# Perceiver megakernel, expert stage: two conditional parts on VectorE joined, and the third transposed group of the first token block issued half a weight group later

## The reference, cut to what matters

```python
scores = softmax(x2d @ gate_w.T)                  # [512, 8]
top_scores, sel = top_k(scores, 2)                # two experts for each of 512 tokens
routed_in = x2d[token_idx] * top_scores           # 1024 rows, sorted by expert
for e in range(8):
    xe = where(eid == e, routed_in, 0)
    h = silu(xe @ w1[e]) * (xe @ w3[e])           # 512 -> 1408
    out += h @ w2[e]                              # 1408 -> 512
x = x + scatter_add(out, token_idx)
```

## Time and profile before

| | |
|---|---|
| time, three runs | median 1844.7 us (1841.14 to 1847.6) |
| profiled execution | 1843.16 us, its span 1841.6 us |
| TensorE busy (matmul) | 1740.0 us, 94% of the span |
| VectorE busy | 1172.4 us, 64% |
| ScalarE busy | 982.1 us, 53% |
| GpSimd busy | 235.9 us, 13% |
| mean granted TensorE clock | 0.977 of full speed |
| expert stage | about 1499.7 to 1825.2 us of the span |

### The profile page before, as it was taken

How to read it: one execution, slowest core, us unless ns; L and a number is a source line. 1 busy time by engine, 2 the same in 40 slices (tenths; PEclk the granted TensorE clock), 3 DMA queues, 4 the chain that set the end, 5 groups by cost and what they waited for, 6 DMA issues and landing times. The chain is left out here.

```text
span 1841.6 us, 25720 instructions
## 1 busy us (share of the span) xinstructions
PE 1740.0 (94%) x9446; PEld 1428.0 (78%) x9446; DVE 1172.4 (64%) x2453; ACT 982.1 (53%) x2033; POOL 235.9 (13%) x138
## 2 busy tenths in 40 slices
PE   7999999999898989999999999999899879999996
PEld 5778888877787779999899989887455557778785
DVE  5777777764534236667677767998434456785753
ACT  6676666642343235556566656887332345665552
POOL 0000000000000022112111211222111022221221
PEclk9999999999999999999999999999899979999998
DMA  6322222217400599778677867667500347786721
GB/s 227 119 104 86 98 81 102 69 69 286 166 1 23 183 290 301 240 225 248 188 234 220 245 188 221 178 197 246 198 6 7 119 165 249 248 299 208 275 65 59
DMA packets 147131, 310.01 MB, mean 168 GB/s; under 512 B 11472, under 2 KB 100816, under 8 KB 135440
## 3 DMA queue, kind: packets, MB, share of 16 engines
q1 hardware_dynamic: 145072, 301.85, 50.1%
q0 software_dynamic: 1920, 6.36, 1.1%
HBM read 226.88 MB, written 81.28 MB: 167 GB/s over the span
## 5 line engine op out<-in xcount | busy, mean ns | idle before, releaser
L1131 ACT CAST PTH<-bank 128x512 fp32r<-128x512 f32 x256 | 149.8, 585 | 164.9 <-PE bank L1126 164.9
L1133 DVE TENSOR_TENSOR PTL<-bank,PTH 128x512 fp32r<-128x512 f32 x256 | 176.0, 687 | 94.9 <-ACT PTH L1131 93.8
L1652 DVE TENSOR_TENSOR WS<-EW,WS 128x1024 fp32r<-128x1024 f32 (+1 forms) x120 | 148.4, 1244 | 80.9 <-ACT WS L1649 78.9
L1111 ACT ACTIVATE TT<-TT,MX 128x512 f32<-128x512 f32 x256 | 186.5, 729 | 8.6 <-DVE MX L1101 8.6
L1083 DVE CUSTOM_DVE_ANT_0 TT<-bank,MASK 128x512 f32<-128x512 f32 x256 | 174.1, 681 | 5.9 <-POOL MASK L1064 5.3
L1649 ACT CAST WS<-EW 128x1024 fp32r<-128x1024 f32 (+1 forms) x144 | 139.1, 977 | 63.3 <-PE bank L1669 62.5
L1126 PE MATMUL bank<-IDN,TT 128*128 128x128 f32 x1024 | 155.2, 274 | 4.0 <-DVE RS L1176 2.9
L101 PE MATMUL bank<-BCH,WKT 128*128 128x256 f32 x512 | 150.6, 294 | 5.2 <-DVE BCL L633 4.4
L102 PE MATMUL bank<-BCL,WKT 128*128 128x256 f32 x512 | 146.9, 287 | 0.0
L103 PE MATMUL bank<-BCH,WKT 128*128 128x256 f32 x512 | 146.8, 287 | 0.0
L1152 PE MATMUL bank<-PTH,VG 128*128 128x256 f32 x512 | 142.6, 300 | 0.2 <-DVE PTL L1133 0.2
(11 more groups left out here) (293 smaller groups left out, 4352.0 us busy)
## 6 DMA issues: line engine op xcount, KB each, us to landing
EW<-in_ewg SPq DMA_DIRECT2D x48, 1024.0 KB, 5.5
KST<-tmp_k SPq DMA_DIRECT2D x43, 768.0 KB, 5.7
tmp_k<-EKH SPq DMA_DIRECT2D x128, 256.0 KB, 2.8
EW<-in_ewg SPq DMA_DIRECT2D x24, 768.0 KB, 4.8
CT<-in_ctxT SPq DMA_DIRECT2D x32, 512.0 KB, 3.2
CN<-in_ctxN SPq DMA_DIRECT2D x32, 512.0 KB, 3.2
BCT<-in_ctxT SPq DMA_DIRECT2D x32, 512.0 KB, 3.5
tmp_k<-EKL SPq DMA_DIRECT2D x64, 256.0 KB, 2.7
```

The costliest lines, as they stand in the source:

```text
L1111: t_e[(n, kc)] = tick("act", act.activation(TT[:, sl, cs], TT[:, sl, cs], ACT.Exp, bias=MX[:, n % 4, 5:6], scale=SC1, accum_out=SUM[:, b % ...
L1131: t = tick("act", act.copy(PTH[:, q], bank[bk][:]))
L1133: t = free[bk] = tick("dve", dve.tensor_tensor(PTL[:, q], bank[bk][:], f(PTH[:, q]), ALU.subtract))
L1652: t_lo = tick(low, E[low].tensor_tensor(WS[:, s, 1, 0:n * w], src, f(WS[:, s, 0, 0:n * w]), ALU.subtract))
```

## The change

Two edits in the expert stage.

1. In `group_one`, the two VectorE conditionals that followed each other at g = 3 and g = 5 (`hidden_dve` of the slice before, and `gate`) become one with both bodies. At g = 1 only the gate stands in it, and at g = 6 only `hidden_dve`, as before. Where block 1 is absent, one drain now raises the semaphore by both amounts. That is 16 conditionals fewer on VectorE, eight of them in short experts.
2. `hidden_zero(2, 7)`, the transposes and the split of the third slice of block 0, is no longer issued behind the second half of g = 6 but behind the first half of g = 7. On TensorE it so comes behind `turn_pe(0, 5)` and behind block 1's work for g = 7; on ScalarE behind the high part of the second half of g = 8 and `gather_act(e + 1, 1)`; on VectorE nothing is passed. No DMA is issued by the step and SyncE's and GpSimd's queues don't hold it.

```diff
             if g in (3, 5, 6):
                 n = (g - 3) // 2 if g < 6 else 2
                 when("act", e, lambda: hidden_act(1, n, 6), ("act1",))
-                when("dve", e, lambda: hidden_dve(1, n, 6), ("dve1",))
+                if g == 6:
+                    when("dve", e, lambda: hidden_dve(1, n, 6), ("dve1",))
             if g in (0, 2, 4):
                 when("act", e, lambda: silu(1, g // 2, bk), ("act1",))
             if g in (1, 3, 5):
-                when("dve", e, lambda: gate(1, g // 2, bk), ("dve1",))
+
+                def hidden_and_gate():
+                    if g > 1:
+                        hidden_dve(1, (g - 3) // 2, 6)
+                    gate(1, g // 2, bk)
+
+                when("dve", e, hidden_and_gate, ("dve1",))
...
             nxt = half_zero(e, 6, 1, a)
-            hidden_zero(2, 7)
             if not last:
                 turn_pe(0, 5, "pe")
             split_half(nxt)
...
             group_one(e, 7, a1)
             nxt = half_zero(e, 7, 0, a)
+            hidden_zero(2, 7)
             split_half(nxt)
```

## The result

The changed kernel takes 1839.16 us (median of 16 runs, 1836.9 to 1844.6), the kernel before 1844.19 us (16 runs, 1841.05 to 1847.6). The ratio is 0.9976, 95% interval 0.9968 to 0.9984: by the ratio 4.4 us less, between 3.0 and 5.9 (the two medians lie 5.0 apart). Forecast were 4.3 us less and 1840.4 us. The profiled execution has a span of 1835.0 us against 1841.6, but 1.5 of these 6.6 us lie ahead of the expert stage, in code that is the same in both.

What follows compares the result with a forecast made beforehand. TensorE bounds long experts; in short ones nothing is full and TensorE waits for VectorE's gate. Gains of 1.6 (e0), 2.8 (e2), 0.45 each (e3, e5), less 1.0 in long experts, give 1844.7 - 4.3 = 1840.4 us; range 1836.5 to 1844.5.

Steps and rivals of the forecast that it cites:

- The place and the sign: TensorE's transposes L1728 wait for VectorE's gate, 6.2 us in four waits, one per short expert; both edits aim there.
- Edit 2 in a short expert: Moved transposes: wait cut from 1.57 to about 0.45 us (for HX), first matmul of g = 7 1.45 us earlier.
- Edit 1 counted at nothing beside edit 2: Joined conditionals bring VectorE's gate 0.58 us earlier, but beside the moved transposes this was counted as no gain.
- The port: At g = 8 GpSimd's memory-port request delays VectorE by 1.1 to 1.3 us, leaving 0.45 of 0.75 us gain.
- The loss in long experts: Moved transposes come later on a never-free TensorE: minus 0.33 us in each long expert except the last.
- The clock: TensorE's clock no longer falls behind the shorter wait in e0 and e2: 1.15 and 1.7 us, 2.85 us together.
- The sum: Whole kernel: e0 1.6, e2 2.8, e3 and e5 0.45 each, long experts -1.0; together 4.3 us less.
- Rival 1: Clock falls behind the shorter wait too, or elsewhere in short experts: 1.5 us left, 1843.2 us; chance 0.20.
- rival 2: VectorE truly bounds short experts, each keeps its saved 0.58 us: 6.6 us, up to 7, 1838.0 us; chance 0.19.
- rival 3: Next weights' cast 1.0 us later against g = 7's first matmul, which moves under 0.7: 4.4 slower, 1849; chance 0.06.

Runs made afterwards that it cites:

- e3: Not a run: a short expert (one block runs) of the expert stage; 30.43 us in the kernel before, 29.59 us in the changed kernel.
- e0: Not a run: a short expert (one block runs) of the expert stage; 34.50 us in the kernel before, 32.54 us in the changed kernel.
- e2: Not a run: a short expert (one block runs) of the expert stage; 31.20 us in the kernel before, 28.47 us in the changed kernel.
- experiment 2: Kernel before with only the transposes moved behind the first half of g = 7, both VectorE conditionals kept; ratio to the kernel before 0.9983.
- e5: Not a run: a short expert (one block runs) of the expert stage; 30.43 us in the kernel before, 29.61 us in the changed kernel.
- experiment 3: Changed kernel, but the transposes move in short experts only and stay at their old place in long ones; ratio to the kernel before 0.9968.
- HX first: Changed kernel, but ScalarE scales the next expert's gathered tokens before the cast of the first half of g = 8; ratio to the kernel before 0.9978.

## Why the prediction was right, point by point

- **The place and the sign: right.** The waits of L1728 for the gate set the time of the short experts, and they are gone.
- **Edit 2 in a short expert: right.** The first matmul of g = 7 was to come 1.45 us earlier against the expert's start; it came 1.42 earlier in e3 with edit 2 alone and 1.56 with both (22.43 against 23.99), where HX is 0.14 earlier too. The wait for HX was forecast at 0.45; it is 0.48 with edit 2 alone and 0.66 with both, since TensorE arrives 0.3 earlier. The wait for XG grew to 0.89 as forecast.
- **Edit 1 counted at nothing beside edit 2: wrong, and the term that was mis-sized.** It gives 0.29 to 0.46 us in each of e0, e2 and e3 there (experiment 2). I had its cover right for the gate, but overlooked two things: the earlier GpSimd result also lets TensorE through g = 5 sooner, and VectorE, 0.6 us ahead at the gate, meets GpSimd's request at g = 8 in another order. Alone it was to give 0.58 in each short expert and gave 0.60.
- **The port: right for edit 2 alone, and decided by 0.03 us with both.** I took 0.45 us for e3 and e5, between 0.35 and 0.75, on the view that GpSimd wins. With edit 2 alone GpSimd did win in e3, VectorE was late for the cast, and e3 gained 0.38. With both edits e3 and e5 gained 0.84 and 0.82, which holds edit 1's part and is not a second error beside it: VectorE's low part started at 1632.00 and GpSimd's request came at 1632.03; VectorE kept the port (1.22), GpSimd waited (2.32 against 1.28 when free), and held up only the next low part, nearly all of which is slack. VectorE was first in all eight short experts of the two profiles of the changed kernel, each time by 0.06 us or less. That the order fell this way, and so steadily, is luck and not something that I had planned. The rule of the Trainium skill (SBUF — State Buffer, SBUF: two separate sides), that whoever starts first holds the pair to its end, was the better guide at g = 8. The 3.12 us row that I set against it stays unexplained. GpSimd's indirect DMA ran until 0.02 us before GpSimd's low part there, but such a DMA under way does not hold VectorE off by itself: as these rows of the kernel before show, two low parts took their usual 0.95 us each, the second from start to end within the DMA at 1627.25. No run isolated what made VectorE wait at 1631.43.

```profile
1626.89 1.82 DVE L1652 TENSOR_TENSOR WS<-EW,WS 128x768 fp32r<-128x768 f32 x2
...
1627.25 2.29 POOL L1702 DMA_INDIRECT HG<-tmp_xd,IDX  x1 [4.51 <-DVE IDX L1700]
...
1630.16 1.42 POOL L1702 DMA_INDIRECT HG<-tmp_xd,IDX  x1 [0.62 <-DVE IDX L1700]
```

- **The loss in long experts: right, a little small.** 0.33 forecast, 0.43, 0.34 and 0.35 measured, and gone when the transposes stay in place (experiment 3).
- **The clock: right in size, its reason open.** 2.85 us were counted for this one profile; 1.15 + 1.55 = 2.7 is what the runs give. Without them the edits give 5.22 - 2.7 = 2.5 us. The kernel before pays 2.7 us in one profile and 1.55 in the other, so about 2 us on average (an estimate from two profiles), and 2.5 + 2 = 4.5 is near what the ratio shows (4.4). Without the clock my sum was 4.3 - 2.85 = 1.45 us. So that 4.3 came out as 4.4 is partly luck: edit 1's part, which I left out, made up for falls of the clock that I counted fully though the kernel before doesn't always have them.
- **The sum.** 4.3 forecast, 5.2 in the profiled stage. e0, e3 and e5 gained 0.36 to 0.39 more than forecast, 1.1 in all and by edit 1; e2 gained 0.07 less and the long experts lost 0.1 more. Rival 1 (clock falls all the same) did not happen in any profile, rival 2 (VectorE's 0.58 in full) came true in half to four fifths of its size, partly by way of the port as it says, and rival 3 (slower) had its delay, 0.65 us between matmul and cast, but not its condition: the matmul moved by 1.56, over twice the 0.7 from which it would have decided.

## What to carry to other kernels

An engine that waits at one step for a slow neighbour can do another step first, but the next thing that it needs decides the gain: here 1.57 us of waiting became 0.66, and the long experts, where TensorE is never free, paid 0.34 to 0.43 us each because the moved step had been filling a gap. Look for that gap wherever the same order serves two cases. And when one instruction is brought forward on an engine, follow what it releases on the others: half of what the joined conditionals gave came through GpSimd's gather and low part, which start behind a signal of VectorE. Time each edit alone: nearly all that both edits save in the stage, edit 1 saves too.

## What the runs showed of the hardware

- A conditional that is not taken costs VectorE 0.28 us even with an empty queue (0.42 against 0.14 between drain and HTL), and the drain in its other branch stops the queue until all earlier work is done (2.57 us in e3).
- The memory port between VectorE and GpSimd is held by whole instructions: with VectorE's start 0.03 us ahead its part took 1.22 and GpSimd's 2.32 us; with GpSimd's 0.03 ahead, GpSimd's took 1.29 and VectorE's 2.34. The order of the recorded starts is no sure sign, though: in the kernel before, a low part of VectorE that began 0.17 us ahead took 3.12.
- The lower clock behind a wait comes and goes between executions of one kernel. It fell in 2 of 4, in 1 of 4, and in 1 of 4 places with a wait nearly twice as long.
- A small gather issued some 9 us ahead can land late when the weight loads keep the DMA engines 90% busy: in e5 ScalarE waited 0.24, 0.31 and 0.70 us for it in three profiles, and not at all at the same place in others. With HX first, when ScalarE asks about 1 us sooner, it waited 1.42, 1.45 and 2.05 us in e3, in every profile of that order.
